# The first fifteen microseconds of a four-layer conditional residual chain: an identity turned on TensorE before any data is there, lora_B loaded in 2 KB pieces, the codebook on another queue, thresholds sorted one step later, and a weight tile turned ahead of the B rows

## The reference, cut to what matters

```python
# layer 0: x += x @ W0.T + b0 + coeff[b] * (x @ (2*mask[b]-1))
# layer 1, weights quantized to a codebook of 8 levels:
lora_delta = lora_B @ lora_A * 0.5                     # lora_B 1024 x 64, lora_A 64 x 1024
cb = codebook / max(|codebook|)
scale = exp(scale_log)                                 # one per row and group of 128 columns
normalized = (weight + lora_delta) / scale
thresholds = (cb[:-1] + cb[1:]) * 0.5                  # seven of them, as sorted by searchsorted
w_q = cb[searchsorted(thresholds, normalized)] * scale
x += x @ (w_q + lora_delta).T
# layer 2: x += x @ W2.T + b2 + 2 * (x @ A2[tok2]) @ B2[tok2]
# layer 3: x += (x @ B3[tok3].T) @ A3[tok3].T
```

## Time and profile before

| | |
|---|---|
| median of 3 runs | 549.89 us (549.53 to 550.72) |
| the profiled execution, its own time | 549.87 us |
| its span in the trace | 548.2 us |
| PE busy | 533.4 us, 97% of the span |
| DVE, ACT, POOL busy | 468.8, 341.7, 192.9 us |

### The profile page before, as it was taken

One profiled execution on the slowest core, in us unless ns is written; L12 is line 12 of the kernel. 1 busy time (PEld: TensorE's weight loads), 2 busy tenths in 40 slices (PEclk: granted clock), 3 DMA queues, 4 the chain that ended last, 5 costly groups with the idle time before them and its releaser, 6 DMA issues.

```text
span 548.2 us, 8917 instructions
## 1 busy us (share of the span) xinstructions
PE 533.4 (97%) x2856; PEld 454.1 (83%) x2856; DVE 468.8 (86%) x723; ACT 341.7 (62%) x658; POOL 192.9 (35%) x179
## 2 busy tenths in 40 slices
PE   5999999999999999999999999999999999999997
PEld 4988888888888787887888788788888878878886
DVE  5998898988865879977999989998997998999862
ACT  3777776776745874586566657557566665755720
POOL 2669867987734020012034204111410420411130
PEclk9999999999999999999999999999999999999999
DMA  8766041843486995558456545645835654664122
GB/s 232 244 92 148 21 125 48 248 138 115 102 186 189 348 326 100 189 157 171 138 161 167 123 160 175 114 155 189 172 134 168 167 126 158 180 103 168 61 59 77
DMA packets 145261, 84.06 MB, mean 153 GB/s; under 512 B 102672, under 2 KB 118032, under 8 KB 145104
## 3 DMA queue, kind: packets, MB, share of 16 engines
q1 hardware_dynamic: 143312, 78.97, 52.4%
q0 software_dynamic: 1632, 4.72, 3.4%
q10 hardware_dynamic: 288, 0.01, 0.0%
HBM read 67.43 MB, written 16.25 MB: 153 GB/s over the span
## 4 chain that ended last, share of the span: by engine, by line
PE 83%; DVE 9%; ACT 4%; DMA 3%; issue 1%; POOL 0%; DVEq 0%; ACTq 0%; SPq 0%; POOLq 0%
PE bank L1637 19%; PE bank L1644 10%; PE bank L1676 7%; PE bank L1677 7%; PE bank L1675 7%; PE bank L1511 5%; PE bank L1513 5%; PE bank L1512 5%; PE bank L1726 3%; PE bank L1725 3%; PE bank L1727 3%; PE bank L1691 3%; PE bank L1421 2%; PE bank L1704 1%; DVE w_lo L1074 1%; DVE merged_ring L1168 1%
## 5 line engine op out<-in xcount | busy, mean ns | idle before, releaser
L1637 PE MATMUL bank<-x_t_pair,m_hi 128*128 128x512 f32 x512 | 128.5, 393 | 1.5 <-ACT m_hi L800 1.4
L800 ACT CAST m_hi<-merged_ring 128x512 fp32r<-128x512 f32 x128 | 73.1, 619 | 60.7 <-PE bank L1644 31.9
L1637 PEld LDWEIGHTS bank<-x_t_pair,m_hi 128*128 128x128 f32 x512 | 92.5, 189 | 19.2 <-ACT m_hi L800 2.3
L1174 DVE TENSOR_TENSOR m_lo<-merged_ring,m_hi 128x512 fp32r<-128x512 f32 x128 | 86.3, 720 | 12.5 <-ACT m_hi L800 12.2
L576 POOL TENSOR_TENSOR x_t_pair<-x_sum,x_t_pair 128x256 fp32r<-128x256 f32 x32 | 29.7, 960 | 179.1 <-ACT x_t_pair L861 179.1
L1168 DVE TENSOR_TENSOR merged_ring<-merged_ring,w_t 128x1024 f32<-128x1024 f32 x64 | 82.1, 1311 | 11.3 <-ACT merged_ring L790 10.3
L790 ACT ACTIVATE merged_ring<-mask_ring,batch_now 128x1024 f32<-128x1024 int32 x64 | 78.0, 1241 | 21.1 <-DMA mask_ring<-in_mask_Bx4096x_ik 20.3
L1644 PEld LDWEIGHTS bank<-x_t_pair,m_lo 128*128 128x128 f32 x512 | 69.8, 190 | 5.0
L1644 PE MATMUL bank<-x_t_pair,m_lo 128*128 128x256 f32 x512 | 71.4, 282 | 0.0
L1676 PE MATMUL bank<-P_lo,x_t_pair 128*128 128x512 f32 x160 | 62.3, 389 | 0.0
L1675 PE MATMUL bank<-P_hi,x_t_pair 128*128 128x512 f32 x160 | 62.3, 389 | 0.0
(11 more groups left out here) (211 smaller groups left out, 1133.5 us busy)
## 6 DMA issues: line engine op xcount, KB each, us to landing
mask_ring<-in_mask_Bx4096x_ik SPq DMA_DIRECT2D x64, 512.0 KB, 4.4
w_nat<-in_L_cond_W SPq DMA_DIRECT2D x14, 512.0 KB, 5.3
x_t_squares<-in_x SPq DMA_DIRECT2D x56, 128.0 KB, 3.0
w_raw<-in_L_cond_weight SPq DMA_DIRECT2D x16, 256.0 KB
out<-out_staged SPq DMA_DIRECT2D x16, 256.0 KB, 4.5
w0t_dram<-w_out SPq DMA_DIRECT2D x14, 256.0 KB, 2.6
g_batch<-g_dram POOLq DMA_DIRECT2D x28, 128.0 KB, 4.3
w_t<-w0t_dram SPq DMA_DIRECT2D x6, 512.0 KB, 5.1
```

Of the source, the lines that this page charges most:

```text
L800: nc.scalar.copy(Mh[:, n % MR], ring_f[:, k % MR, h * HALF:(h + 1) * HALF]).then_inc(s["h_set"], 1)
L1174: nc.vector.tensor_tensor(Ml[:, n % MR], ring_f[:, k % MR, h * HALF:(h + 1) * HALF], Mh[:, n % MR].bitcast(F32), ALU.subtract).then_inc(s[ ...
L1637: mm(bank[L0_BANK[HT * h + j]][:, :], Mh[:, n % MR, j * P:(j + 1) * P], xThl[:, :, :, k + i, :], start=(k + i == 0), stop=False, skip_grou ...
```

## The change

Five edits, all within the opening:

1. PE runs 14 transposes of the identity into PSUM bank 0 as soon as the identity is there, before it waits for lora_B.
2. lora_B is read as `(p t) r` where it was `(t p) r`: partition p takes eight neighbouring rows, one run of 2 KB, where it took eight runs of 256 B. The turned columns then come out in another order, and ACT's write into `lbt` puts them back with a stride of eight elements.
3. The codebook's load moves from SP's queue (third there) to ACT's queue, behind the two token lists.
4. DVE's eleven instructions for steps, thresholds and their sort move from before `add_delta(0)` to behind it.
5. `w2_transpose(1)` goes ahead of the two `b3_transpose` on PE; on ACT `w2_hi(1)` and `mid_up(0)` go ahead of `b3_set(0)` and `b3_set(1)`.

```diff
-            sp.dma_start(lbn[:, :, :], lora_b.rearrange("(t p) r -> p t r", p=P)).then_inc(s["lora_b_in"], 16)
+            sp.dma_start(lbn[:, :, :], lora_b.rearrange("(p t) r -> p t r", t=KT)).then_inc(s["lora_b_in"], 16)
             sp.dma_start(la[0:RL, :], lora_a).then_inc(s["lora_a_in"], 16)
-            sp.dma_start(cb[:, :], row(codebook).broadcast_to([P, NCB])).then_inc(s["cb_in"], 16)
...
+            act.dma_start(cb[:, :], codebook.rearrange("(o n) -> o n", o=1).broadcast_to([P, NCB])).then_inc(s["cb_in"], 16)
...
-                nc.scalar.mul(lbt[0:RL, h * 512:(h + 1) * 512], bank[5 + h][0:RL, :], L1_SCALE).then_inc(s["lbt_set"], 1)
+                spread = lbt[0:RL, :].rearrange("r (p t) -> r t p", t=KT)[:, h * HT:(h + 1) * HT]
+                nc.scalar.mul(spread, bank[5 + h][0:RL, :].rearrange("r (t p) -> r t p", p=P), L1_SCALE).then_inc(s["lbt_set"], 1)
...
             inner_up(0)
+            w2_hi(1)
+            mid_up(0)
             b3_set(0)
             b3_set(1)
-            w2_hi(1)
-            mid_up(0)
...
-            step.did(nc.vector.tensor_tensor(dd[:, :], cb[:, 1:NCB], cb[:, 0:NTH], ALU.subtract))
-            link(nc.vector.tensor_tensor(th[:, :], cb[:, 1:NCB], cb[:, 0:NTH], ALU.add))
...
             add_delta(0)
+            step.did(nc.vector.tensor_tensor(dd[:, :], cb[:, 1:NCB], cb[:, 0:NTH], ALU.subtract))
+            link(nc.vector.tensor_tensor(th[:, :], cb[:, 1:NCB], cb[:, 0:NTH], ALU.add))
...
             pe.wait_ge(s["ident_set"], 1)
+            for _i in range(WARM):
+                nc.tensor.transpose(bank[0][:, 0:P], ident[:, :], ident[:, :])
             pe.wait_ge(s["lora_b_in"], 16)
...
             w2_transpose(0)
+            w2_transpose(1)
             b3_transpose(0)
             b3_transpose(1)
-            w2_transpose(1)
             v_part(0)
```

More of the change, by code:

```diff
@@ L277, in cond_resid_chain @@
         MISC = 7
+        WARM = 14
         @block.sync
@@ L1096, in _, with c @@
             add_delta(0)
+            step.did(nc.vector.tensor_tensor(dd[:, :], cb[:, 1:NCB], cb[:, 0:NTH], ALU.subtract))
+            link(nc.vector.tensor_tensor(th[:, :], cb[:, 1:NCB], cb[:, 0:NTH], ALU.add))
+            link(nc.vector.tensor_scalar(th[:, :], th[:, :], 0.5, None, ALU.mult))
+            def c(i):
+                return th[:, i:i + 1]
+            step.did(nc.vector.tensor_tensor(c(1), c(1), c(3), ALU.min))
+            link(nc.vector.tensor_tensor(c(5), c(5), c(3), ALU.max))
+            step.did(nc.vector.tensor_tensor(c(0), c(0), c(1), ALU.min))
+            step.did(nc.vector.tensor_tensor(c(2), c(2), c(1), ALU.max))
+            step.did(nc.vector.tensor_tensor(c(4), c(4), c(3), ALU.max))
+            link(nc.vector.tensor_tensor(c(6), c(6), c(5), ALU.max))
+            step.did(nc.vector.tensor_tensor(c(2), c(2), c(3), ALU.min))
+            link(nc.vector.tensor_tensor(c(4), c(4), c(5), ALU.min))
             nc.vector.tensor_scalar(cs[:, :, :], sc[:, :, :], cb[:, 0:1], None, ALU.mult).then_inc(s["first_level"], 1)
```

## The result

The changed kernel takes 553.05 us, the median of 10 runs (551.17 to 554.09); the kernel before, on the same chip, takes 550.25 (549.53 to 550.77, 10 runs). The ratio is 1.0044, 95% interval 1.0031 to 1.0057: 2.8 us slower by the medians and 2.4 (1.7 to 3.1) by the ratio. I had forecast 551.1 and a range up to 552.3. The direction was right, but the slowdown is more than twice the 1.24 us of the sum, and the range did not hold it. The ten runs scatter over 2.9 us, where the ten of before scatter over 1.2; over more sessions the kernel before scatters as widely (549.46 to 552.66 in 103 runs), so the scatter by itself says little.

What follows compares the result with a forecast made beforehand. PE, busy 97% of the span, was taken as the bound, reached through a chain handing over at 61.89. Delay 2.59 less 1.35 gained gives +1.24 us on the 549.89 median: 551.1 us, range 548.6 to 552.3.

Steps and rivals of the forecast that it cites:

- the sum: Opening: PE's chain 2.59 us late less DVE's 1.35 gained, +1.24 us carried to the end, 551.1 us.
- The chain through v_part(0) without slack: PE and ACT beside DVE's path: whatever delays v_part(0) delays effective(0); 1.24 us late.
- PE stands idle meanwhile, since W2's tile 2 is written behind v_part(0): PE ahead of v_part(0): it waits for the B rows' copies, with tile 2's transposes queued behind.
- Of the 1.35 us won nothing reaches effective(0): DVE at w2_lo(2): the earlier terms_a(0) is lost waiting; effective(0) comes at 27.4 instead of 26.15.
- the cover that I gave the first delta: PE to DVE at add_delta(0): first delta ready 0.7 us before DVE wants it, so no wait.
- the falling clock: PE's two new gaps of about 2 us: the clock falls, 1.9 us more, 553.0 us; chance 0.05.
- The cold-transposes rival: PE's opening: identity transposes don't raise the clock, deltas stay cold, DVE gains 0.50, 552.0 us; chance 0.13.
- The rival that the forward shift passes through: Chain through v_part(0): hidden room lets DVE's 1.35 us reach 61.89, 548.5 us; chance 0.17.
- No slack seen up to effective(0), dense from there: From v_part(0) to 61.89 and the end: the +1.24 us delay passes on in full.

Runs made afterwards that it cites:

- the filled pauses: Kernel after the change, plus 12 identity transposes in PE's pause ahead of tile 1 and 14 ahead of v_part(0): 551.50 us, ratio 1.0023.
- the run with the old order and a filled pause: Kernel after the change with edit 5 undone, plus 16 identity transposes on PE in the pause ahead of the B rows: 550.53 us, ratio 1.0005.
- one line of ACT's order: Kernel after the change with only ACT's mid_up(0) put back behind b3_set(1), PE's order kept: 550.30 us, ratio 1.0008.

## Why the prediction was right in direction and wrong in size

**Right, with its numbers.** The chain through v_part(0) without slack is what decided. The sum has v_part(0) 1.24 us late, at 17.77; it was 17.88, 1.35 late, and with edit 5 alone 2.55 against 2.59. "PE stands idle meanwhile, since W2's tile 2 is written behind v_part(0)": shown by moving tile 2, which alone took 553.05 to 550.39 (550.84 for the runs with a fall, so most of it is not the clock's). "Of the 1.35 us won nothing reaches effective(0)": nothing did. lora_B landed in 3.7 us instead of 4.81, 1.1 us earlier where the prediction had up to 0.9.

**Right by luck in part.** terms_a(0) at 12.02 (11.79 in the sum) is made of misses that nearly cancel. The codebook's first instruction came at 6.51 and not 7.13, since the tokens' row numbers, which I had left where they were, were done 0.98 us earlier. But the cover that I gave the first delta was not there: ACT's strided write took 1.0 us a half against 0.59, inside its bound, the deltas started at 7.76, and DVE waited 0.68 us for the first of them (add_delta(0) at 9.00, 8.85 in the sum).

```profile
9.00 0.69 DVE L963 TENSOR_TENSOR w_raw<-w_raw,bank 128x512 f32<-128x512 f32 x1 [0.68 <-PE bank L1424]
```

The thresholds then took 1.64 us against 1.34.

**The step that failed** is the one that gave the falling clock a chance of 0.05 and left it out of the sum. I wrote that "the longest pause before was 1.15 and left the rate high", and that the change opens two pauses of about 2 us, and priced the fall at 1.9 us and 553.0. The right reading was that nothing in the trace of before speaks for a clock that stays up in pauses twice as long. Measured, PE paused 1.69 and 2.28 us, the fall came in 10 of 10 runs, and in 5 of 5 with edit 5 alone. In the profile it costs 1.65 us of PE; over the runs, 1.5 between pauses open and filled (553.05 - 551.50, across two sessions), and 1.4 between runs of the kernel before with and without one (551.42 - 550.03). That the kernel before itself has a fall in one run of seven couldn't be seen in its one profile. With the rival's price the sum is 551.1 + 1.9 = 553.0. That this meets the measured median is luck in part, as two more terms were missing and nearly cancel: about 0.8 us is given back between effective(0) and w2_lo(4), and 0.73 is lost again after the hand-over. How the 2.8 us of the medians divide between order and clock is not settled by the runs: among runs with a fall, the changed kernel is 2.45 us above the same with edit 5 undone (553.05 and 550.60), while the filled pauses leave 1.2 for the order.

**The given-back 0.8 us** was in the trace of before and I read over it. The path of before holds an instruction of DVE, L1043, that adds a 128x128 identity in 1.35 us while POOL sums terms:

```profile
26.87 1.35 DVE L1043 TENSOR_TENSOR acc<-acc,ident 128x128 f32<-128x128 f32 x1
```

```profile
26.78 1.28 POOL L523 TENSOR_TENSOR pooled<-pooled,term_b 128x512 f32<-128x512 f32 x1
```

The same instruction took 0.29 after the change. In all six profiled executions in which it starts more than 0.04 us before the end of such a sum (L523), it ends 0.15 to 0.16 us behind POOL's: before, DVE until 28.22 and POOL until 28.06. So a late DVE misses that collision and gets 0.8 to 1.1 us back. "No slack seen up to effective(0), dense from there" was wrong by this.

**The cold-transposes rival fell in the profiled execution**, and with it the page's rule. With 14 identity transposes and lora_B's eight directly behind them, and no other matmul before, the deltas took 2.02 us instead of 3.75, from their first instruction on. It was so in seven of the eight profiles with edits 1 and 2. The Trainium skill, "TensorE: Matmul & The Clock Gate", Part 4, PE-mode transpose, says that transposes don't count as busy in the way matmuls do; by that rule the deltas would have been cold, and the trace disagrees for these fp32 transposes.

**The rival that the forward shift passes through** (0.17) was not the case: v_part(0) had no room. What would be won if it did is in the run with the old order and a filled pause: 1.10 us at the hand-over, and nothing at the end.

**Open.** Why a pause of 2.1 to 2.4 us brings the clock down in half of the runs of one kernel and in all of another; how long the pauses were is known for one run of each. Why runs without a fall still scatter over 2 us and more, in the kernel before (549.46 to 551.80) as in that with both pauses filled (550.38 to 553.47). What the 1.4 us are that come with the fillers. Why the part from the hand-over to the end varies between 486.2 and 488.8 us was only traced to its waits: `m_hi`, and with fillers and an early hand-over a load of W0 that takes longer to land (6.4 and 5.8 us against 4.4). No version was tried that keeps the forward shift with short pauses and without fillers.

## What to carry to other kernels

An edit that makes TensorE finish early work sooner can open a pause, and a pause has a price of its own: look for the longest pause that the trace before shows with the clock still up, and treat a longer one as likely to cost a stretch at half rate, not as a rarity; the mean clock of each run then tells whether it did. Filling a pause with work that nobody reads kept the clock up in most runs here, and in only one of four kernels did it clearly win time. When a late instruction is moved behind something, look at what stands behind it in the same queue: here one line of ACT's order, or one tile moved ahead of the waiting matmuls, was worth 2.7 us. A step with an unusually long duration on the old path (1.35 us for a 128x128 add) can be slack in disguise, since a shift can dissolve it.

## What the runs showed of the hardware

A DVE addition whose operands all lie in SBUF waited for a POOL elementwise operation that was running: the 128x128 add took 0.29 us in the eight profiles in which no such operation ran beside it, or only its last 0.04 us; in the other six it took 0.57 to 1.35 and ended 0.15 to 0.16 us behind POOL's, each time. In the kernel after, a DVE minimum over one column, 0.15 us else, took 0.40 and ended at 10.74, while a POOL addition ran from 10.28 to 10.73:

```profile
10.34 0.40 DVE L1092 TENSOR_TENSOR thresholds<-thresholds 128x1 f32<-128x1 f32 x1
```

```profile
10.28 0.45 POOL L514 TENSOR_TENSOR w_nat<-w_nat,ident 128x128 f32<-128x128 f32 x1 [2.71 <-DMA w_nat<-in_L_cond_W]
```

In the seven profiles with a fall, the granted clock went down anywhere between 0.5 us ahead of the end of a pause (edits 3 and 4 alone: 15.0, PE back at 15.52) and 1.0 us behind it (the changed kernel: 18.9, PE back at 17.88), and then stayed at 0.50 for 3.4 us each time, with PE at work for most of it (18.9 to 22.3 in the changed kernel). ACT's write with a stride of eight fp32 elements took 1.0 us for 512 columns, the contiguous one 0.59.
